# Expert biases of the last stage, expert weight loads and small tables moved in a twelve-stage decoder kernel on one core

## The reference, cut to what matters

```python
# last cross-attention, 16 heads of 16, distance penalty (ALiBi) added to the scores
x = layernorm(x + (softmax(q @ k.T * scale - slope * distance) @ v) @ Wo + bo)

# last feed-forward: per token t
logits = x @ Wg.T                              # 8 experts
top2, idx = top_k(logits, 2); p = softmax(top2)
h = gelu(x @ W1[e] + b1[e])                    # 256 -> 1024, for e in the two experts of t
y = sum_i p[i] * (h_i @ W2[idx[i]] + b2[idx[i]])
out = layernorm(x + y)
```

## Time and profile before

| what | us |
|---|---|
| median of three runs | 3452.08 |
| the profiled execution's own time | 3451.57 |
| its span in the trace | 3449.8 |
| PE busy in the span | 2849.0 |
| DVE busy in the span | 1914.0 |
| block of `finish` in the last cross-attention | 2993 to 3017 |
| block of `route_tokens` | 3017 to 3090 |
| block of `run_experts` | 3090 to 3395 |
| last block | 3395 to the end |

### The profile page before, as it was taken

The page is one execution under the profiler, slowest core; times in us unless marked ns, Lnnn a source line. Parts: engine busy times, 40 slices in busy tenths (PEclk is TensorE's granted clock), DMA queues, the critical chain, the costliest instruction groups (busy, mean ns, idle before and its releaser), DMA issues. The chain is left out here.

```text
span 3449.8 us, 53931 instructions
## 1 busy us (share of the span) xinstructions
PE 2849.0 (83%) x18533; PEld 1729.9 (50%) x18565; DVE 1914.0 (55%) x4654; ACT 1588.8 (46%) x4360; POOL 690.0 (20%) x774
## 2 busy tenths in 40 slices
PE   6586894845999999768987988989888979959993
PEld 3443562322555555435654663446633455539992
DVE  6547675343778877476746662156523548733333
ACT  4313682312777777483134652135521539803331
POOL 3201011030211210011205550045500003301113
PEclk9686997977999999889998999999999989959996
DMA  1000002010000000100000001000000000051112
GB/s 69 1 2 14 1 2 80 0 55 12 1 1 2 1 2 12 49 5 9 6 21 29 1 3 58 0 7 1 1 28 12 7 22 2 2 226 34 36 35 81
DMA packets 34789, 80.46 MB, mean 23 GB/s; under 512 B 8577, under 2 KB 23570, under 8 KB 30450
## 3 DMA queue, kind: packets, MB, share of 16 engines
q1 hardware_dynamic: 29746, 64.61, 5.2%
q0 software_dynamic: 4368, 11.93, 1.2%
q10 hardware_dynamic: 432, 0.80, 0.1%
HBM read 63.31 MB, written 14.02 MB: 22 GB/s over the span
## 5 line engine op out<-in xcount | busy, mean ns | idle before, releaser
L2459 ACT ACTIVATE scores<-scores,min 128x128 f32<-128x128 f32 (+7 forms) x256 | 198.5, 775 | 86.0 <-DVE min L2442 82.1
L2440 DVE TENSOR_SCALAR zero_marks<-psum 128x128 f32<-128x128 f32 (+7 forms) x256 | 192.0, 750 | 66.6 <-PE psum L2372 64.8
L2442 DVE CUSTOM_DVE_ANT_0 scores<-psum,zero_marks 128x128 f32<-128x128 f32 (+7 forms) x256 | 193.9, 757 | 29.9 <-issue 0.9
L2379 PE MATMUL psum<-ident,scores 128*128 128x128 f32 x1152 | 172.8, 277 | 16.5 <-ACT probsT L2476 13.4
L2476 ACT ACTIVATE probsT<-psum 128x128 f32<-128x128 f32 (+7 forms) x256 | 163.0, 637 | 31.7 <-PE psum L2379 30.9
L3707 PE MATMUL psum<-Hn,W 128*128 128x512 f32 x384 | 169.3, 604 | 8.8 <-PEq L415 8.8
L1597 ACT ACTIVATE XT<-psum,b_of_tile 128x128 f32<-128x128 f32 x312 | 89.0, 368 | 180.3 <-PE psum L1517 180.3
L1517 PE MATMUL psum<-x_gatheredT,XT 128*128 128x128 f32 x1248 | 153.5, 283 | 6.2 <-issue 3.3
L1517 PEld LDWEIGHTS psum<-x_gatheredT,XT 128*128 128x128 f32 x1248 | 148.3, 198 | 14.6 <-issue 13.4
L2379 PEld LDWEIGHTS psum<-ident,scores 128*128 128x128 f32 x1152 | 123.2, 141 | 55.9 <-issue 30.3
L2369 PE MATMUL psum<-XT,Q_heads 64*128 64x512 f32 x256 | 143.7, 641 | 0.0
(11 more groups left out here) (619 smaller groups left out, 6807.0 us busy)
## 6 DMA issues: line engine op xcount, KB each, us to landing
W<-in_L3f_W SPq DMA_DIRECT2D x16, 1024.0 KB, 22.4
L3f_y_rows<-y SPq DMA_DIRECT2D x39, 128.0 KB, 1.7
L0f_rows<-Xtok SPq DMA_DIRECT2D x2, 2048.0 KB, 8.1
W<-in_L0f_W SPq DMA_DIRECT2D x3, 1152.0 KB
early_weights<-in_L2f_Wqkv SPq DMA_DIRECT2D x2, 1536.0 KB
W<-in_L2f_W SPq DMA_DIRECT2D x2, 1536.0 KB
XT<-in_xT SPq DMA_DIRECT2D x1, 2048.0 KB, 10.2
Xtok<-in_xtok SPq DMA_DIRECT2D x1, 2048.0 KB
```

Source lines behind the costliest of these rows:

```text
L2379: ins = pe.transpose(turned[:, kt * P:(kt + 1) * P], Sc[:, i % ROT, kt * P:(kt + 1) * P], K.ident[:])
L2440: dve.tensor_scalar(zero[:, i % 2, 0:n], sc(i)[:, 0:n], 0.0, -NEG, ALU.is_equal, ALU.mult)
L2442: dve.tensor_tensor_reduce(Sc[:, i % ROT, 0:n], sc(i)[:, 0:n], zero[:, i % 2, 0:n], 1.0, -NEG, ALU.add, ALU.min, low[:, i % ROT:i % ROT + ...
L2459: act.activation(p, p, ACT.Exp, bias=low[:, i % ROT:i % ROT + 1], scale=-1.0, accum_out=sums[:, u % 2, h:h + 1]).then_inc(s["exp_done"], 1)
```

## The change

- In `finish` of the last cross-attention SP also issues `Wg` and `b2` (through `K.ahead`) and then six of the eight W1 blocks. The place of W1 is taken ahead of that block (`hold_experts`); the load counts on a semaphore made at the start of the program.
- In `route_tokens` SP issues the store to `x_rows` first, then the two remaining W1 blocks, the eight W2 blocks and `b1`, and at its end waits for the store. PE waits for `K.late` in place of the loads of its own block. The expert biases are gone from PE, ACT and DVE there; the sum of the gates goes to a small table that lives on.
- In the last block PE makes the 16 transposes, four tiles to a bank, and then the 16 products with b2, two tiles to each of four banks; ACT copies four tiles at once; DVE adds groups 0 and 1 ahead of the first gathered group, group 2 between statistics and normalisation of group 0, group 3 in the same place of group 1.
- Small tables of routing and of the experts' buffers move into the region of early weights and the buffer of the context; the output of the cross-attention (`OT`) goes into the input buffer of that stage, which is no longer read then; the distance table moves inside. Nothing in these moves adds or removes an instruction.

```diff
@@ finish
             for dst, src in K.ahead:
                 sp.dma_start(dst, src).then_inc(K.late, 16)
+            for e in K.experts_ahead:
+                issue_expert(sp, K, w, 0, e)
@@ early_loads
+    if sublayer is L3_ffn:
+        return ((early_gate(K), w["L3f_Wg"]), (early_b2(K), w["L3f_b2"]))
@@ cross_attention
-        OT = sbuf(es, nc, "OT", [P, DC, TOK])
+        OT = K.XT[K.cur]
...
-        finish(nc, K, lambda k, t: Wo[:, k, :], tile_of_block(OT), DC, bias=bo[:])
+        if alibi:
+            hold_experts(nc, K)
+        finish(nc, K, lambda k, t: Wo[:, k, :], tile_of_block(OT), DC, bias=bo[:], w=w)
+        K.experts_ahead = ()
@@ new
+EARLY_EXPERTS = 6
+def hold_experts(nc, K):
+    K.expert_life = ExitStack()
+    K.expert_W1 = sbuf(K.expert_life, nc, "W1", [P, EXPERTS * EW])
+    K.expert_W2 = None
+    K.experts_ahead = tuple(range(EARLY_EXPERTS))
+def issue_expert(eng, K, w, part, e):
+    if part == 0:
+        eng.dma_start(K.expert_W1[:, e * EW:(e + 1) * EW].rearrange("p (k n) -> p k n", k=DC), w["L3f_W1"][e]).then_inc(K.weights_in, 16)
+    else:
+        eng.dma_start(K.expert_W2[:, e * EW:(e + 1) * EW].rearrange("p (m n) -> p m n", m=IC), w["L3f_W2"][e]).then_inc(K.weights_in, 16)
@@ L3_ffn, last block
+            @block.tensor
+            def _(pe):
+                for t in range(NT):
+                    ins = pe.transpose(K.bank[t // GT][0:EXPERTS, (t % GT) * P:(t % GT + 1) * P], gates_sum[:, t, :], K.ident[:])
+                    if t % GT == GT - 1:
+                        ins.then_inc(s["turned"], 1)
+                for t in range(NT):
+                    pe.wait_ge(s["turned_out"], t // GT + 1)
+                    if t >= 8:
+                        pe.wait_ge(s["bias_out"], 2 * (t // 2) - 6)
+                    pe.matmul(bias_bank(t), gT[:, t, :], b2, start=True, stop=True).then_inc(s["bias_done"], 1)
...
+                def add_bias(k):
+                    for t in groups[k]:
+                        dve.wait_ge(s["bias_done"], 2 * (t // 2) + 2)
+                        dve.tensor_tensor(K.Xtok[:, t, :], bias_bank(t), K.Xtok[:, t, :], ALU.add).then_inc(s["bias_out"], 1)
...
+                add_bias(0)
+                add_bias(1)
                 for k, tiles in enumerate(groups):
+                    dve.wait_ge(s["bias_out"], (k + 1) * GT)
                     dve.wait_ge(gathered[k], 16 * 2 * GT)
...
                     last.then_inc(s["stats_done"], 1)
+                    if k + 2 < len(groups):
+                        add_bias(k + 2)
                     normalise(k)
@@ route_tokens
-                sp.dma_start(Wg[:], w["L3f_Wg"]).then_inc(s["loaded"], 16)
-                sp.dma_start(b2[:], w["L3f_b2"]).then_inc(s["loaded"], 16)
                 sp.dma_start(x_rows.rearrange("(t p) d -> p t d", p=P), K.Xtok[:]).then_inc(s["x_stored"], 16)
+                for e in range(EARLY_EXPERTS if ready else 0, EXPERTS):
+                    issue_expert(sp, K, w, 0, e)
                 for e in range(EXPERTS):
-                    sp.dma_start(W1[...], w["L3f_W1"][e]).then_inc(weights_in, 16)
-                    sp.dma_start(W2[...], w["L3f_W2"][e]).then_inc(weights_in, 16)
+                    issue_expert(sp, K, w, 1, e)
                 sp.dma_start(b1[:], w["L3f_b1"]).then_inc(weights_in, 16)
+                sp.wait_ge(s["x_stored"], 16)
...
-                pe.wait_ge(s["loaded"], 32)
+                pe.wait_ge(K.late, K.late_count)
...
-                pe.wait_ge(s["gates_done"], 1)
-                for t in range(NT):
-                    if t >= 2:
-                        pe.wait_ge(s["turned_out"], t - 1)
-                    pe.transpose(K.bank[1 + t % 2][0:EXPERTS, 0:P], gates[:, 0, t, :], K.ident[:]).then_inc(s["turned"], 1)
-                    if t >= 2:
-                        pe.wait_ge(s["bias_out"], t - 1)
-                    pe.wait_ge(s["turned_out"], t + 1)
-                    pe.matmul(K.bank[3 + t % 2][:, 0:D], gT[:, t % 2, :], b2[:], start=True, stop=True).then_inc(s["bias_done"], 1)
                 pe.wait_ge(s["hot_done"], 1)
...
-                dve.wait_ge(s["x_stored"], 16)
-                for t in range(NT):
-                    dve.wait_ge(s["bias_done"], t + 1)
-                    dve.tensor_tensor(K.Xtok[:, t, :], K.bank[3 + t % 2][:, 0:D], K.Xtok[:, t, :], ALU.add).then_inc(s["bias_out"], 1)
                 dve.wait_ge(s["found"], 1)
```

More of the change, by code:

```diff
@@ L1260, in _ @@
             def _(act):
+                for k in range(len(groups)):
+                    act.wait_ge(s["turned"], k + 1)
+                    act.activation(gT[:, k * GT:(k + 1) * GT, :].rearrange("e t k -> e (t k)"), K.bank[k][0:EXPERTS, :], ACT.Copy).then_inc(s["turned_out"], 1)
                 for k in range(len(groups)):
@@ new lines, in route_tokens @@
+        ints = left.take("p n -> p n", P, I32)
+        token_ints = left.take("p (i t) -> p i t", 2 * NT, I32, i=2)
+        num = left.take("p n -> p n", P)
+        place = left.take("p (i t) -> p i t", 2 * NT, i=2)
+        L = left.take("p (t e) -> p t e", NT * EXPERTS, e=EXPERTS)
+        top = left.take("p (t e) -> p t e", NT * 8, e=8)
+        at = left.take("p (t e) -> p t e", NT * 8, U32, e=8)
+        atf = left.take("p (t e) -> p t e", NT * 8, e=8)
+        one = left.take("p (i t e) -> p i t e", 2 * NT * EXPERTS, i=2, e=EXPERTS)
@@ new lines, in route_tokens @@
+        gates = left.take("p (i t e) -> p i t e", 2 * NT * EXPERTS, i=2, e=EXPERTS)
+        chosen = left.take("p (t e) -> p t e", NT * EXPERTS, e=EXPERTS)
+        upto = left.take("p (i t e) -> p i t e", 3 * NT * EXPERTS, i=3, e=EXPERTS)
+        tiles = left.take("p (i e) -> p i e", 4 * EXPERTS, i=4)
+        sl = left.take("p (a i t) -> p a i t", 3 * 2 * NT, a=3, i=2)
+        passed = left.take("p (g e) -> p g e", SLOT_TILES * EXPERTS, e=EXPERTS)
+        found = left.take("p (i g) -> p i g", 3 * SLOT_TILES, i=3)
```

113 lines of the change are left out of this document (59 added, 54 removed).

## The result

The changed kernel takes 3429.78 us (median of four runs, 3428.33 to 3433.72) against 3454.09 for the kernel before on the same chip (also four runs now): ratio 0.993, interval 0.9913 to 0.9947. It gains 24.3 us; the prediction said 30.5 (3421.3, at most 3428). The profiled execution has a span of 3426.6 us.

A forecast was written before the change was run, and what follows sets the result against it. Bound by a chain of waits: in routing the bias queue ahead of the one-hot products, at the end POOL's gathers. 2.3 + 28.3 - 0.1 = 30.5 us off 3451.6 gave 3421.3 us, range 3417 to 3428.

The forecast's parts named there:

- Wait for `Wg` and b2: Start of `route_tokens`: requesting both early lets PE start at once, gaining 2.3 us (1.5 to 2.4).
- bias queue out of routing: Routing: one-hot products no longer stand behind the bias rounds, gaining 28.3 us (28.0 to 28.4).
- Weights are next and early: Before the first W1 copy: weights land about 3051, 12 us early, cost nothing; rival that they bound, 3425, chance 0.07.
- Traffic slows nothing: `finish`, now with 15 us of transfers: engines not slowed, cost 0, up to 0.5 us.
- Clock: TensorE at the experts' first multiplications: removing the bias work from routing leaves the clock's pattern unchanged, cost 0.
- this rival: First expert steps meet the other clock level: 3418.4 if it rises early, 3427.8 if late; chance 0.12, half each.
- The last block: Added bias work there delays group 3 by 0, at most 4.0 us; rival that it becomes late, 3425, chance 0.07.
- all bounds together: Whole kernel: the terms' bounds summed, a gain of at least 24.4 and at most 33.7 us.
- POOL under the additions: Last block: gathers slowed under the new additions, cost 0.1 us, bounds 0 to 0.6.
- The base: Profile of the kernel before: execution of 3451.6 us, 0.5 below the median of three runs, its last block's timings used.
- The sign that I had named: Last block: DVE's last group starts 43.3 us after the first gather, as before, if the forecast is right.
- the other one: Last block: group 3 waiting for nothing, named as a sign that the forecast is wrong.

The follow-up runs named there:

- prefetch0: Changed kernel with none of the six W1 blocks requested early in `finish`, all sixteen weight blocks requested in the routing block; 3429.75 us.
- no_bias: Changed kernel without any expert-bias work in the last block, biases left out of the output; last block 56.7 us against 64.3 in again.
- pairs: Changed kernel with 8 bias additions of 512 columns in place of 16 of 256; last block 61.8 us.
- bias_routing: Changed kernel with the bias work put back into routing, all else kept; stalls of 7.3 us in all in the last block.
- again: The changed kernel unchanged, profiled once more; last block 64.3 us, same stalls in group 1.
- half_gathers: Changed kernel with its whole bias work but 16 gathers of y rows in place of 32; last block 47.0 us, one stall of 2.92 us.
- pause_tail: Changed kernel with a pause of 18.87 us on VectorE between expert loop and last block; last block as long, stalls begin at the same distance.
- dve_only: Changed kernel keeping VectorE's 16 additions in the last block, without transposes, copies or products; median 3428.40 us, 2.7 us over the 56.7 us block.
- pe_only: Changed kernel keeping TensorE's and ScalarE's bias work in the last block, VectorE's 16 additions left out; median 3426.49 us, last block 61.5 us.
- pe_quiet: As pe_only, but the 16 products set no semaphore mark; last block 60.0 us.
- before_again: The kernel before the change, unchanged, profiled a second time; last block 56.7 us, with stalls.
- split_adds: Changed kernel with bias products in TensorE's wait for one-hot tables, additions in routing and around the first gather, none in the last block; 3422.47 us, ratio 0.9910.

## Why the prediction missed

- *Wait for `Wg` and b2, bias queue out of routing:* right. 30.8 us measured for 30.6.
- *Weights are next and early:* right. Traffic ends at 3050 (forecast 3051). The prefetch was called worth at most 4.1; it moves the first W1 copy by 5.4, since the first gathered tile too comes late while the weights move (7.0 instead of 3.5 us, prefetch0), which I had left out, and 1.5 us reach the end in one profile, none in the medians.
- *Traffic slows nothing:* right for this profile; `finish` took 24.1 us as before, and the block of routing even began 1.4 us earlier, which other executions don't repeat (3017.04 to 3023.38). In two later profiles with the early weights, no_bias and pairs, `finish` took 26.4; why isn't known.
- *Clock:* right for the profiled execution, yet "0" hides that the experts come out near 305 or near 302 us, in no_bias, pairs and bias_routing the latter. In pairs it was the second multiplication up, 3.83 us. The profiles differ by 3 to 4 us through it. The prediction gave this rival a chance of 0.12; that the first profile had the old pattern is luck in part.
- *The last block:* here the step failed. "0 is what I take", with 4.0 as the bound, counted VectorE's and TensorE's own work and the room ahead of group 3. That arithmetic held: group 0 started even earlier than I had it. Missing was a cost that falls on neither: while the gathers run, additional instructions on TensorE and ScalarE, or on VectorE, make VectorE stand still at drains and ScalarE's root come late. It measures 7.6 us (no_bias against again; 5.4 to 7.6 with the other profiles of that code), where the sum had 0 and the bound 4.0. Although the other terms came out at their forecast or above it, the gain of 24.3 lies just under the 24.4 that all bounds together gave.
- *POOL under the additions:* 0.1 was taken. All gathers that ran beside the first eight additions (y0 + 4 to y0 + 10) took 0.95 us, so it is 0; the three longer ones ran beside the additions of gathered rows.
- *The base:* 54.0 for the old last block was one execution's. The usual one is 56.7. By profiles the block got 9.5 us longer; 2.7 of these are this difference. If the median of before already contains the small stalls, as five of six profiles suggest, the gain is 30.8 - 7.6 = 23.2 and some tenths, and 24.3 was measured. The time itself is 8.5 us above the 3421.3 of the forecast: 6.2 are gain that did not come, 2.0 that the median of before went from 3452.08 to 3454.09 with a fourth run, the rest rounding.
- *The sign that I had named,* group 3 starting 43.3 us after y0, did show it: 52.8. So did the other one, group 3 waiting for nothing: it has no idle time ahead of it.

What stays open is the mechanism under the stalls. Shown is: the long ones need more than the first sixteen gathers of y rows (half_gathers), they come within the block and not from what went ahead (pause_tail), start earlier the more other instructions run beside the gathers (no_bias, dve_only, pe_only, the full work: y0 + 35, 29, 28, 24 to 26), hardly depend on the products' marks (pe_quiet), end 3 to 6 us after the last gather is issued, and those at drains are no wait for rows, for POOL or for a bank. Nor are they a wait for instructions to be loaded, as far as the profile records that: each of the sixteen profiles has one such transfer in its last block, after the stalls (y0 + 53.1 in the changed kernel), and the profile without stalls has it too (y0 + 46.1).

One thing goes with the stalls in all sixteen profiles. The transfers of the last block, 32 gathers and 4 stores, set 16 landing marks each, 576 in all. The first profile of before, the only one without stalls, has all 576; before_again has 236 and the changed kernel 143. The marks thin out long before the first stall: of some 64 per 5 us, 18 are recorded from y0 + 15 to y0 + 25 in before_again, and 8 to 10 from y0 + 10 to y0 + 30 in the changed kernel. (half_gathers lacks marks as well, 124 of 320, and has its one stall.)

The missing marks and the stalls fit a queue of events, the profiler's records included, which backs up to the engines; a run without recording was not made, so whether the stalls exist without it isn't known, and with it not how much of the 7.6 us an unrecorded execution would pay. The Trainium skill (NOTIFIC — the notification-queue block, "7.1 Overflow: three behaviours, one of which stalls the engine") says that a full queue of such records does one of three things, as it is set: it drops the new record, overwrites the oldest, or holds its producer until it is drained. Held producers would stand still the sooner the more they have to record, as here; lost records would leave marks missing, as here. No run here shows the queue itself or how it was set.

## What to carry to other kernels

- Work moved "beside" a stage of many small gathers is not free because the engines are idle there; count its instructions as well as their time, and prefer idle time without such traffic, as split_adds did (4.6 to 5.4 us less for the same work by the profiles; the rest of its 7.3 us goes with the shorter experts).
- A stretch on which a forecast rests needs a second profiled execution: 54.0 and 56.7 were the same code.
- After shortening a quiet stage, look which transfers now overlap with the first small transfer behind it, not only whether the big ones are in time.

## What the runs showed of the hardware

- In the recorded executions VectorE stood still 15.4 us in a stretch of 19 beside small gathers, 12.6 of them at drains with nothing to wait for and 2.8 for a root of ScalarE that started 3.8 us late (changed kernel), while POOL kept its pace of 1.25 to 1.36 us per gather but for one of 1.48.
- TensorE's granted clock at the start of the experts came out in several ways: the first two multiplications up took 6.44 and 6.78 us (the changed kernel), 5.50 and 3.83 (prefetch0), 5.34 and 3.83 (pairs), 5.34 and 5.46 (split_adds), where 3.83 is the time at 2.4 GHz. In the 18 to 21 us ahead of the one-hot products TensorE had been busy 1.4 us in the changed kernel, 1.2 in prefetch0 and 2.4 in pairs, and 14.2 in split_adds. No rule is drawn from it.
